# Operand stacks of a split-precision attention laid out batch, row, head, token in DRAM and SBUF; parts written one by one; output weights loaded with the constants

## The reference

```python
q, k, v = (xn @ W.T for W in (Wq, Wk, Wv))        # 16 heads of 16, then rope on q and k
gate = einsum('bshd,bnhd->bhsn', q, mean of k over blocks of 32)
sel  = top-4 blocks of gate, own block always, future blocks never
scores = where(sel and causal, q @ k.T * 16**-0.5, -1e30)
o = softmax(scores) @ v
s = (o * rsqrt(mean(o*o) + eps) * o_norm_w) @ Wo.T
g = experts(xn) + shared(xn)                      # 8 experts, top 2, hidden 176; shared hidden 352
x = x + s * silu(g)
```

## Time and profile before

| | |
|---|---|
| median of the runs | 444.06 us (443.27 to 444.36) |
| the profiled execution's own time | 442.4 us |
| its span, first to last instruction | 440.6 us |
| mean granted clock of TensorE | 0.918 |
| PE, DVE, ACT, POOL busy | 351.2, 301.3, 170.8, 172.7 us |
| DMA | 30.20 MB in 23066 packets |
| packets of SP's queue (q1) | 19003, 18.80 MB |
| packets of ACT's queue (q10) | 4032, 11.01 MB |

### The profile page before, as it was taken

The page is one execution under the profiler, slowest core; times in us unless marked ns, Lnnn a source line. Parts: engine busy times, 40 slices in busy tenths (PEclk is TensorE's granted clock), DMA queues, the critical chain, the costliest instruction groups (busy, mean ns, idle before and its releaser), DMA issues. The chain is left out here.

```text
span 440.6 us, 6052 instructions
## 1 busy us (share of the span) xinstructions
PE 351.2 (80%) x2028; PEld 242.6 (55%) x2028; DVE 301.3 (68%) x857; ACT 170.8 (39%) x305; POOL 172.7 (39%) x119
## 2 busy tenths in 40 slices
PE   0795875858606998999999999999963789898782
PEld 0584563745305665766566666665763568344641
DVE  3867599849608786789354664676575967838794
ACT  1422723712002432223444444545220484975710
POOL 5653551643205463255426555465426400000032
PEclk9999889789955998999999999999978599999898
DMA  8100299979891332111211114111003400000011
GB/s 277 33 26 9 71 156 175 159 204 126 177 117 36 84 74 45 45 65 37 80 37 37 36 39 132 36 38 35 1 2 94 159 0 1 0 1 0 1 48 48
DMA packets 23066, 30.20 MB, mean 69 GB/s; under 512 B 3171, under 2 KB 18187, under 8 KB 23035
## 3 DMA queue, kind: packets, MB, share of 16 engines
q1 hardware_dynamic: 19003, 18.80, 22.0%
q10 hardware_dynamic: 4032, 11.01, 8.4%
HBM read 24.99 MB, written 4.82 MB: 68 GB/s over the span
## 5 line engine op out<-in xcount | busy, mean ns | idle before, releaser
L380 POOL TENSOR_TENSOR wl<-wr,wh 128x768 fp32r<-128x768 f32 x28 | 51.2, 1827 | 71.5 <-ACT wh L466 55.2
L522 ACT ACTIVATE PT<-bank 128x512 f32<-128x512 f32 (+1 forms) x88 | 44.3, 558 | 39.5 <-PE bank L946 39.4
L679 DVE TENSOR_REDUCE mx<-bank 128x1 f32<-128x384 f32 (+3 forms) x88 | 52.4, 636 | 7.9 <-PE bank L927 7.6
L925 PE MATMUL bank<-KS,QS 112*128 112x128 bf16 (+3 forms) x128 | 34.5, 323 | 27.7 <-DVE mx L679 22.1
L149 PE MATMUL bank<-xh,wh 128*128 128x512 f32 x112 | 51.3, 458 | 4.0 <-DVE gb L804 1.4
L418 POOL TENSOR_TENSOR gl<-gb,gh 128x512 fp32r<-128x512 f32 x28 | 36.4, 1300 | 37.6 <-DVE gh L811 25.0
L790 DVE SCALAR_TENSOR_TENSOR s<-th,bank 128x512 f32<-128x512 f32 x28 | 19.2, 685 | 40.0 <-ACT th L529 40.0
L150 PE MATMUL bank<-xl,wh 128*128 128x512 f32 x112 | 46.0, 410 | 0.0
L151 PE MATMUL bank<-xh,wl 128*128 128x512 f32 x112 | 45.6, 407 | 0.0
L1207 POOL TENSOR_TENSOR left<-xn,x 128x256 f32<-128x256 f32 x8 | 7.0, 896 | 85.1 <-DVE xn L1434 85.1
L149 PE MATMUL bank<-wh,gh 128*128 128x256 f32 x112 | 37.6, 336 | 0.5 <-POOL gl L418 0.5
(11 more groups left out here) (233 smaller groups left out, 825.0 us busy)
## 6 DMA issues: line engine op xcount, KB each, us to landing
wr<-in_w_chunks_dram ACTq DMA_DIRECT2D x28, 384.0 KB, 3.2
QS<-parts_dram SPq DMA_DIRECT2D x12, 256.0 KB
KS<-parts_dram SPq DMA_DIRECT2D x12, 256.0 KB, 8.6
parts_dram<-wp SPq DMA_DIRECT2D x4, 384.0 KB, 3.5
parts_dram<-x SPq DMA_DIRECT2D x4, 384.0 KB, 14.9
w_ai<-in_w_ai_dram SPq DMA_DIRECT2D x1, 1152.0 KB, 5.8
x<-in_x_dram SPq DMA_DIRECT2D x2, 512.0 KB, 6.5
KS<-in_x_dram SPq DMA_DIRECT2D x1, 1024.0 KB, 5.6
```

The source lines that it names most:

```text
L380: pool.tensor_tensor(wl[:, s % 3, :, :], wr[:, s % 2, :, :], wh[:, s % 3, :, :].bitcast(F32), ALU.subtract).then_inc(wl_ready, 1)
L522: act.activation(PT[:, k % 8, 0:n], bank[k % 2][:, 0:n], ACT.Exp, scale=float(DH) ** -0.5).then_inc(P_ready, 1)
L679: dve.tensor_reduce(mx[:, b * TB + i, heads[0]:heads[-1] + 1], bank[k % 2][:, 0:len(heads) * n].rearrange("p (h n) -> p h n", n=n), AX.X, ...
L925: pe.matmul(out, QS[0:R_MAX, h, b * S + i * P:b * S + (i + 1) * P], KS[0:R_MAX, h, b * S:b * S + n], start=True, stop=False)
```

## The change

Four things change. (1) The stacks get the shape batch, head, token behind the row, in SBUF and in DRAM, so that what one partition receives in a read-back is one run of 16 KB at both ends, where it was 16 runs of 1 KB from places 16 KB apart. (2) For the queries the copies of a row group are read back as three DMAs of 48, 32 and 16 rows (parts 0 to 2, parts 0 to 1, part 0) instead of six DMAs of 16 rows; the keys stay at six DMAs of 16 rows. The stack's order of pairs follows from this, and the set of six pairs is the same. (3) Each part of a piece is written by a DMA of its own as soon as it is there (three writes a piece instead of one), and the bias in two writes instead of one; their DRAM side now runs over 8 heads first. The constant rows of `KS` come in two loads, one a batch. (4) `wo` has a buffer of its own, and its load is issued after the small constants and before the constant rows of `KS`.

```diff
-        QS = m.sb("QS", [P, H, T * P], BF16)
-        KS = m.sb("KS", [P, H, T * P], BF16)
+        QS = m.sb("QS", [P, B, H, S], BF16)
+        KS = m.sb("KS", [P, B, H, S], BF16)
...
+        wo = early.sb("wo", [P, KD, D])
         early_ctx.close()
...
-        wo = PT[:, 0, :].rearrange("p (k n) -> p k n", n=D)
...
-        parts_dram = nc.dram_tensor("parts_dram", (B, 2, 3, D, S), BF16, kind="Internal").ap()
-        bias_dram = nc.dram_tensor("bias_dram", (B, D, S), BF16, kind="Internal").ap()
+        parts_dram = nc.dram_tensor("parts_dram", (B, 2, 3, DH, H, S), BF16, kind="Internal").ap()
+        bias_dram = nc.dram_tensor("bias_dram", (B, NBLK, H, S), BF16, kind="Internal").ap()
...
-            sp.dma_start(KS[R_BIAS:R_ALL, :, :], spread(a["c_kconst"], 1, H)).then_inc(kconst_ready, 16)
+            sp.dma_start(wo[:, :, :], a["w_o"].rearrange("(k p) n -> p k n", p=P)).then_inc(sem_wo, 16)
+            for b in range(B):
+                sp.dma_start(KS[R_BIAS:R_ALL, b, :, :],
+                             spread(a["c_kconst"][:, b * S:(b + 1) * S], 1, H)).then_inc(kconst_ready, 16)
 
             def stack_bias(b):
                 sp.wait_ge(biasT_read, b + 1)
-                sp.dma_start(bias_dram[b].rearrange("(f p) t -> p f t", p=P),
-                             biasT[:, :, :]).then_inc(bias_out, 16)
-                sp.wait_ge(bias_out, 16 * (b + 1))
-                sp.dma_start(QS[R_BIAS:R_MAX, :, b * S:(b + 1) * S],
-                             bias_dram[b].rearrange("(h n) t -> n h t", n=NBLK)).then_inc(q_stacked[b], 16)
+                for f in range(2):
+                    sp.dma_start(bias_dram[b, :, f * 8:(f + 1) * 8, :].rearrange("n h t -> h n t"),
+                                 biasT[:, f, :]).then_inc(bias_out, 16)
+                sp.wait_ge(bias_out, 32 * (b + 1))
+                sp.dma_start(QS[R_BIAS:R_MAX, b, :, :], bias_dram[b]).then_inc(q_stacked[b], 16)
 
             def stack_parts(b, halves):
                 for k in halves:
                     n = 4 * b + k
                     which, half = k // 2, k % 2
-                    sp.wait_ge(H_ready, n + 1)
-                    sp.wait_ge(M_ready, n + 1)
-                    sp.wait_ge(L_ready, n + 1)
-                    sp.dma_start(parts_dram[b, which, :, half * P:(half + 1) * P, :].rearrange("l p t -> p l t"),
-                                 parts[n % 4]).then_inc(parts_out[n % 4], 16)
+                    for level, done in enumerate((H_ready, M_ready, L_ready)):
+                        sp.wait_ge(done, n + 1)
+                        sp.dma_start(parts_dram[b, which, level, :, half * 8:(half + 1) * 8, :].rearrange("d h t -> h d t"),
+                                     parts[n % 4][:, level, :]).then_inc(parts_out[n % 4], 16)
                     if half == 0:
                         continue
 
-                    sp.wait_ge(parts_out[(n - 1) % 4], 16 * (b + 1))
-                    sp.wait_ge(parts_out[n % 4], 16 * (b + 1))
-                    dst, done = ((QS, q_stacked), (KS, k_stacked))[which]
-                    for r, pair in enumerate(STACK):
-                        sp.dma_start(dst[r * DH:(r + 1) * DH, :, b * S:(b + 1) * S],
-                                     parts_dram[b, which, pair[which]].rearrange("(h d) t -> d h t", d=DH)
-                                     ).then_inc(done[b], 16)
+                    sp.wait_ge(parts_out[(n - 1) % 4], 48 * (b + 1))
+                    sp.wait_ge(parts_out[n % 4], 48 * (b + 1))
+                    src = parts_dram[b, which].rearrange("l d h t -> (l d) h t")
+                    row = 0
+                    for first in range(3):
+                        count = 3 - first
+                        rows = slice(row, row + count * DH)
+                        if which == 0:
+                            sp.dma_start(QS[rows, b, :, :], src[0:count * DH]).then_inc(q_stacked[b], 16)
+                        else:
+                            for r in range(row, row + count * DH, DH):
+                                sp.dma_start(KS[r:r + DH, b, :, :], src[first * DH:(first + 1) * DH]
+                                             ).then_inc(k_stacked[b], 16)
+                        row += count * DH
...
             stack_parts(1, range(4))
 
-            sp.dma_start(wo[:, :, :], a["w_o"].rearrange("(k p) n -> p k n", p=P)).then_inc(sem_wo, 16)
             stack_bias(1)
...
-                    pe.matmul(out, QS[0:R_MAX, h, b * S + i * P:b * S + (i + 1) * P],
-                              KS[0:R_MAX, h, b * S:b * S + n], start=True, stop=False)
+                    pe.matmul(out, QS[0:R_MAX, b, h, i * P:(i + 1) * P], KS[0:R_MAX, b, h, 0:n], start=True, stop=False)
```

More of the change, by code:

```diff
@@ L288, in unit_of @@
             return u // (NG * TB), (u // TB) % NG, u % TB
-        xr = KS[:, 4:12, 0:S].bitcast(F32)
-        yth = QS[:, 0:8, 0:S].bitcast(F32)
-        sq = KS[:, 0, 0:S].bitcast(F32).rearrange("p (i h d) -> p i h d", i=TB, d=DH)
+        xr = KS[:, 0, 4:12, :].bitcast(F32)
+        yth = QS[:, 0, 0:8, :].bitcast(F32)
+        sq = KS[:, 0, 0, :].bitcast(F32).rearrange("p (i h d) -> p i h d", i=TB, d=DH)
         block = ctx.enter_context(nc.Block())
@@ L344, in stack_maxima @@
                 sp.wait_ge(max_out, 16 * (b + 1))
-                sp.dma_start(QS[R_MAX:R_ALL, :, b * S:(b + 1) * S],
+                sp.dma_start(QS[R_MAX:R_ALL, b, :, :],
                              max_dram[b].rearrange("(l h) t -> l h t", l=3)).then_inc(q_stacked[b], 16)
@@ L394, in slot @@
                         if n >= 4:
-                            pool.wait_ge(parts_out[n % 4], 16)
+                            pool.wait_ge(parts_out[n % 4], 48)
                         pool.tensor_tensor(parts[n % 4][:, 2, :], R1[:, n % 2, :], parts[n % 4][:, 1, :],
@@ L470, in bias_rows @@
                 if b:
-                    act.wait_ge(bias_out, 16)
+                    act.wait_ge(bias_out, 32)
                 act.copy(biasT[:, :, :].rearrange("p f t -> p (f t)"), bank_b[2][:, :]).then_inc(biasT_read, 1)
@@ L498, in slot @@
                         if n >= 4:
-                            act.wait_ge(parts_out[n % 4], 16)
+                            act.wait_ge(parts_out[n % 4], 48)
                         act.wait_ge(X_ready, n + 1)
@@ L913, in scores_by_query @@
                 if g == 0 and r == 0:
-                    pe.wait_ge(q_stacked[b], 16 * (len(STACK) + 1))
+                    pe.wait_ge(q_stacked[b], 16 * (3 + 1))
                     pe.wait_ge(k_stacked[b], 16 * len(STACK))
-                    pe.wait_ge(kconst_ready, 16)
+                    pe.wait_ge(kconst_ready, 16 * B)
                 i, heads = unit_loads(g)[r]
@@ L936, in scores_by_key @@
                 if w % NG == 0 and r == 0:
-                    pe.wait_ge(q_stacked[b], 16 * (len(STACK) + 2))
+                    pe.wait_ge(q_stacked[b], 16 * (3 + 2))
                 if k == 0:
@@ L943, in scores_by_key @@
                     out = bank[k % 2][:, o * n:(o + 1) * n]
-                    pe.matmul(out, KS[0:R_ALL, h, b * S + j * P:b * S + (j + 1) * P],
-                              QS[0:R_ALL, h, b * S + j * P:(b + 1) * S], start=True, stop=False)
+                    pe.matmul(out, KS[0:R_ALL, b, h, j * P:(j + 1) * P], QS[0:R_ALL, b, h, j * P:S], start=True, stop=False)
                     ins = pe.matmul(out[:, 0:P], ident_b[:, :], tri[:, 1, :], start=False, stop=True)
```

## The result

The changed kernel takes 425.62 us, the median of four runs (424.02 to 427.33), against 443.66 us for the kernel before (442.56 to 444.36, four runs). The ratio is 0.9603 with a 95% interval of 0.9569 to 0.9638. The forecast was 427.9 us in a range of 421 to 433.5.

What follows compares the result with a forecast made beforehand. Two stretches waiting for stack traffic (late `wo` before step 7, batch 0's bias rows) were taken as the bound; 13.5 + 1.0 + 1.7 = 16.2 us off 442.4 gives 426.2, plus 1.7 for the median: 427.9 us, range 421 to 433.5.

Steps and rivals of the forecast that it cites:

- The wait for `wo`: Before step 7: the early load lets PE's end at 118.88 release the tanh, not 132.42; 13.5 us saved.
- The clock in step 7: Step 7: without the stop PE keeps its full clock; 1 us saved, bounds 0 and 2.
- the kernel behind that: Layer 0's second pass and layer 1: same work in the same tiles, only shifted; cost 0.
- Batch 0's chain: Stack traffic before batch 0's first scores: they come at 93.9 instead of 95.59; 1.7 us saved, bounds 4.8 and -2.6.
- the writes' +1.7: Batch 0, pieces 2 and 3: writes over 8 heads take 4.0 us instead of 2.3.
- 0.5 as the sign: During the stack writes: a DMA share near 0.5 if they run on 8 engines, near 1 if not.
- Queries nearer to full rate, keys not: Batch 0's read-backs: queries 8.7 us instead of 13.0, above 150 GB/s; keys stay at 13.0, near 121.
- Covers: Batch 1's stacks and bias stay hidden, cost 0; step 9's weights might come late, 0 to 1.5 us, taken as 0.
- Rival 1: Stack read-backs: keys become fast too, scattered DRAM places being the cause; 423.8 us, chance 0.25.
- rival 4: Step 7: something else holds it and the wait stays; 434 us if half the stop came back, chance 0.05.
- Rival 2: Only `wo` gains: batch 0 2.6 us later, no clock gain, step 9's weights 1.5 late; 434.7 us, chance 0.12.
- Rival 3: Large read-backs run on few engines; on three, first scores at 115 and 449 us; chance 0.03.

Runs made afterwards that it cites:

- Experiment 1: The kernel before with only wo in its own buffer and loaded early, stacks as before: 426.13 us, ratio 0.9583.
- experiment 2: The changed kernel with wo again in PT's first buffer, loaded behind batch 1's stacks: 442.86 us, ratio 0.9964.
- the second timing of the changed kernel: The changed kernel unaltered, timed again on one chip beside experiment 4's kernel: 425.9 us, six runs, ratio 0.9597.
- experiment 6: Experiment 3's kernel with parts and bias in the DRAM order of the kernel before: 426.35 us, ratio 0.9559.
- experiment 5: The changed kernel with keys in three loads, row order unchanged, the repetition outermost in the source: 455.36 us, ratio 1.0205.
- experiment 3: The changed kernel with queries read back in six loads of 16 rows, runs still 16 KB: 429.32 us, ratio 0.9653.
- experiment 4: The changed kernel with stack rows ordered feature first, copy second, and keys in three loads too: 422.81 us, timed again 421.87 us.
- Experiment 7: Experiment 4's kernel with all four pieces of a batch written before the first read-back: 431.77 us, ratio 0.9692.

## Why the prediction was right

The mechanism was right: one late load held the whole core, and an early one frees it. The nearness of the total, 16.2 us forecast and 18.2 measured in the profiled execution, is partly luck, since the errors of the terms had both signs. The 18.2 us split as follows. Removing the stop gives 17.2: the tanh of step 7 comes 16.6 us sooner after that of step 6, step 7 is 1.6 shorter and step 8 1.0 longer. Experiment 1, with this load alone, measures the same by medians, 443.4 - 426.1 = 17.3. Step 10 is 1.45 shorter, which is not the stop's doing (below). The stacks give 1.15 up to step 6, and 1.77 are lost because this execution had fallen behind by the second tanh (55.85 against 54.08). These add up to 18.1 (16.63 + 1.59 - 0.98 + 1.45 + 1.15 - 1.77).

**The wait for `wo`: right mechanism, mis-sized.** Forecast 13.5 us, measured 16.1 for DVE, which is the next to be held. The prediction took the matmul that ends at 118.88 for the gate product of step 7, which releases the tanh. It is the up product. Two rows of the trace of before show it: six matmuls of the gate product end here, and the end of the up product is followed by the product with `ksel`.

```profile
115.36 0.40 PE L151 MATMUL bank<-xh,wl 128*128 128x512 f32 x1
...
118.81 0.39 PE L1007 MATMUL bank<-combT,ksel 64*128 64x512 bf16 x1
```

So ACT could have begun at 115.8, and DVE, done with its row maxima at 116.98, was the next to be ready: 133.04 - 116.98 = 16.1, the longest wait of DVE for the tanh in the list of waits before. In the changed kernel the tanh comes 16.01 us earlier in absolute time (132.42 - 116.41), although the step before it was 0.62 late (106.15 against 105.53), and it starts right behind the end of the gate product, 116.38. "PE still had 5 us of work under it" was the failed sentence: the up product doesn't hold the tanh.

**The clock in step 7.** Forecast 1.0, measured 1.6 (11.93 to 10.34 us from tanh to tanh). The granted clock is 1.00 from 118 to 130 in the changed kernel; before it was at 0.50 from 138 to 142 with PE nearly full. The two kernels with the stop take 11.93 and 11.85 us for this step (before and experiment 2), those of experiment 1 and the change 10.36 and 10.34; that the clock accounts for all of it was not tried by itself. Step 8 then takes 8.47 us against 7.49 and gives 1.0 back, a term that the prediction did not have. Step 10 is 1.45 shorter (10.16 against 11.61), but it takes 10.16 in experiment 2 as well, which keeps the stop. In the profiled execution of the kernel before the granted clock was 0.50 from 168 to 170 us, and it was 1.00 through this step in those of experiments 1 and 2, so this part of the 18.2 is an accident of that execution. From there to the end the two traces keep the same distance within 0.1 us, as forecast under "the kernel behind that".

**Batch 0's chain.** Forecast 1.7 us saved. The parts of the sum in the profiled execution: queries out to keys out -2.6, where the queries' -4.3 and the writes' +1.7 gave the same -2.6; keys out to bias read +1.4, forecast +0.9. The exact match is luck: in the other executions with these stacks (the second timing of the changed kernel, and experiment 2) the first distance is 15.85 and 18.06 us, so -4.1 and -1.9, and with the stacks of before it is 19.92 us in the kernel before and 20.31 in experiment 1. That the writes run on half the engines shows in the DMA share of 0.54 with 192 GB/s from 98 to 99 us, against 1.07 with 373 GB/s in experiment 6, where they run over 128 rows; the prediction had named 0.5 as the sign. The rule of the Trainium skill's page DMA: Bandwidth & Descriptors that the prediction weighed, the largest divisor up to 16 of the slowest dimension of both sides, fits this and experiment 5. The first scores nevertheless come at 96.21, later than 95.59, because the execution was 1.78 us late before the first read-back. That lag is not the change's: in the other profiled execution of the same kernel (of its second timing) the queries go out at 57.06, as before, and the first scores are these:

```profile
93.39 0.23 PE L933 MATMUL bank<-KS,QS 112*128 112x128 bf16 x1 [3.32 <-DMA QS<-bias_dram]
```

2.2 us before those of the kernel before, from the same start; that execution took 421.49 us. What makes the start differ is in the section on the hardware. So the term had the right sign where the start is the same, and within the scatter of the medians it can't be seen (experiment 2).

**Queries nearer to full rate, keys not.** Right in kind: the keys' 131 GB/s is near the forecast 121, and with the queries in six loads of 16 rows the keys go out 4.3 us later behind them (21.57 against 17.29, experiment 3), which is what the prediction gave the three loads. The queries' own rate, for which it named 150 GB/s as the sign, can't be read from a window, since weights and writes run in the same stretch. Experiments 3 and 4 show that merging the rows decides, not the length of the runs. The port map of the Trainium skill's page SBUF — State Buffer (section "SBUF: two separate sides") fits: loads of 16 rows on few ports are slow at either length of run, and the merged loads, which reach more ports by it, are faster.

**Covers.** Batch 1's stacks and bias were hidden, as forecast; no wait for step 9's weights came up. The weights that ACT waited 3.44 us for in the kernel before cost 0.5 us now. Experiment 7 shows how thin that cover is elsewhere.

**Rivals.** Rival 1 failed in experiment 3, rival 4 in experiment 1. Rival 2 failed in its time, 434.7 us, which had the stacks 2.6 us slower and no gain in clock; but its headline, that only `wo` gains, is nearest to what experiments 1 and 2 show, and the forecast's 1.7 us for the stacks is the term that no median confirms. Rival 3 did not happen to this kernel and did, in one transfer, to experiment 5: first scores at 114.31, for which the prediction had said 115 on three engines. That the two agree is chance, since the prediction put all of the stack traffic on three engines and experiment 5 only the keys' first two loads on few.

## What to carry to other kernels

Look first for the one transfer that sits behind a queue of others and is needed by an engine that leads all the rest: giving `wo`, 2 KB a partition, a place of its own bought 17 of the 18 us (experiment 1), and the rewriting of the stacks next to nothing by itself. When a load is to be split or merged, look at its outermost dimension on both sides and at how many target rows it reaches before looking at the length of its runs. And before reordering transfers, see which transfer of another engine's queue uses the gap that is closed.

## What the runs showed of the hardware that was not expected

**A load on ACT's queue waits for what SP has queued.** In experiment 7 the 384 KB issued at 62.90 are there only 21 us later. SP's read-backs of queries, 1.57 MB, were issued just before them, from 61.28, and those of keys, as much again, just after, from 63.28. Two issuing queues were no help against that backlog, not even, it seems, against the part of it that came later. The kernels that read queries in six loads of 16 rows wait for the same weights too, 3.4 us before and 3.3 to 4.1 in experiments 1, 3 and 6, and the changed kernel 0.5. How the two queues are served was not tried by itself.

**Scatter from the first 25 us.** Runs of the changed kernel go from 421.5 to 427.7 us. Two profiled executions of the same kernel differ by 1.0 us already at the first tanh (39.84 and 38.79) and by 1.8 at the second (55.85 and 54.01). In the slower one matmuls of the first projection still take 0.63 us, where the trace of before, which starts like the faster one, has 0.39 (the faster one has 0.40 at 20.35):

```profile
20.44 0.63 PE L151 MATMUL bank<-wp_h,xl 128*128 128x512 f32 x1
```

```profile
20.40 0.39 PE L151 MATMUL bank<-wp_h,xl 128*128 128x512 f32 x1
```

The windows call the granted clock 1.00 in both there. Yet 0.63 us is also what a matmul of this size takes at 142.73 in the trace of before, where the granted clock was 0.50 (142 to 143 us). What sets the slower pace at the start stays open; no experiment tried it. From 40 to 50 us the granted clock differs as well, 0.66 in the slower execution and 0.83 in the faster. The two spans end 2.7 us apart (422.4 and 419.7), of which 1.8 are there at the second tanh. That is as much as the effects of the stacks, and is why experiment 4 was timed twice.
